# Three-layer graph network with a sign-split feed-forward stage: who fetches the last 128 rows of each group in layer 2, and who takes the signs

## The reference

```python
x = x + gnn(layernorm(x), edges, edge_type, W_rel, W_root, bias)
#   for l in range(3):
#       msg = einsum('nd,rde->rne', x, W_rel[l])[edge_type, src]
#       x = relu(segment_sum(msg, dst) + x @ W_root[l] + bias[l])
x = x + ffn(layernorm(x), weight, bias)
#   lx, lw = log(|x| + 1e-8), log(|w| + 1e-8);  mx, mw = their row maxima
#   log_out = log(exp(lx - mx) @ exp(lw - mw).T) + mx + mw.T
#   out = sign(sign(x) @ sign(w).T) * exp(log_out) + bias
```

## Time and profile before

| what | us |
|---|---|
| three timed runs | 5857.26, 5858.69, 5864.41 (median 5858.69) |
| profiled execution: time, span | 5867.15, 5865.4 |
| POOL busy | 4326.9 (74%) |
| PE busy | 4266.2 (73%) |
| VectorE busy | 1827.4 (31%) |
| ACT busy | 619.3 (11%) |

### The profile page before, as it was taken

How to read it: one execution, slowest core, us unless ns; L and a number is a source line. 1 busy time by engine, 2 the same in 40 slices (tenths; PEclk the granted TensorE clock), 3 DMA queues, 4 the chain that set the end, 5 groups by cost and what they waited for, 6 DMA issues and landing times.

```text
span 5865.4 us, 124620 instructions
## 1 busy us (share of the span) xinstructions
PE 4266.2 (73%) x26040; PEld 3874.6 (66%) x26041; DVE 1827.4 (31%) x3534; ACT 619.3 (11%) x848; POOL 4326.9 (74%) x4573
## 2 busy tenths in 40 slices
PE   3777777777777677777777777767777777777776
PEld 2766767666666566666666666656666666666666
DVE  4222222222222222222222222223333333334334
ACT  3010110101010010000000001001111111101111
POOL 4777777777777677777777777767777777777775
PEclk7999999999999898999999999989888888888898
DMA  6444444444444343444343334333334334333332
GB/s 194 116 117 116 118 117 116 117 117 117 117 117 116 108 114 112 113 113 113 112 113 113 113 112 114 112 103 113 113 113 115 113 112 114 113 113 113 113 113 85
DMA packets 314263, 674.98 MB, mean 115 GB/s; under 512 B 96052, under 2 KB 168217, under 8 KB 313850
## 3 DMA queue, kind: packets, MB, share of 16 engines
q0 software_dynamic: 218256, 596.28, 35.9%
q1 hardware_dynamic: 54580, 42.39, 2.5%
q10 hardware_dynamic: 41014, 32.79, 1.8%
HBM read 645.39 MB, written 25.68 MB: 114 GB/s over the span
## 4 chain that ended last, share of the span: by engine, by line
POOL 31%; PE 25%; issue 19%; SPq 13%; DMA 6%; DVEq 3%; DVE 2%; ACTq 1%; ACT 1%; POOLq 0%
POOL rows L452 31%; PE bank L473 14%; SPq L366 10%; PE bank L550 10%; DMA rows<-node_table,idx 5%; SPq L292 3%; DVEq L1110 1%; DVEq L1107 1%; DVE agg L1124 1%; ACTq L768 1%; DVEq L1214 1%; PE bank L689 0%; ACTq L292 0%; ACT agg L811 0%; ACT x_in L735 0%
## 5 line engine op out<-in xcount | busy, mean ns | idle before, releaser
L452 POOL DMA_INDIRECT rows<-node_table,idx x4547 | 4319.5, 950 | 1489.3 <-issue 1327.9
L473 PE MATMUL bank<-onehot,rows 128*128 128x128 f32 x18212 | 2658.6, 306 | 1227.7 <-DVE agg L1124 560.0
L473 PEld LDWEIGHTS bank<-onehot,rows 128*128 128x128 f32 x18212 | 2508.9, 218 | 1368.5 <-issue 1350.3
L1124 DVE TENSOR_TENSOR agg<-bank,agg 128x256 f32 x1566 | 664.0, 424 | 2111.6 <-PE bank L473 1578.8
L550 PE MATMUL bank<-wrel,agg 128*128 128x256 f32 x5568 | 1270.5, 387 | 16.5 <-issue 12.7
L550 PEld LDWEIGHTS bank<-wrel,agg 128*128 128x128 f32 x5568 | 1074.0, 196 | 167.5 <-issue 22.1
L1027 DVE TENSOR_TENSOR onehot<-bank,key 128x1152 f32<-128x1152 f32 x525 | 707.2, 1347 | 0.2
L811 ACT COPY agg<-zero_col 128x2304 f32 x174 | 367.2, 2111 | 2832.4 <-PE bank L550 1608.5
L1146 DVE SCALAR_TENSOR_TENSOR acc<-bank,in_first,acc 128x256 f32 x174 | 84.2, 484 | 1808.1 <-PE bank L550 1684.7
L818 ACT COPY acc<-bank 128x256 f32 (+1 forms) x98 | 36.5, 373 | 1224.9 <-issue 974.7
L663 PE MATMUL bank<-ident,new_x 128*128 128x128 f32 x196 | 43.1, 306 | 128.1 <-ACT new_x L869 128.1
(11 more groups left out here) (140 smaller groups left out, 864.2 us busy)
## 6 DMA issues: line engine op xcount, KB each, us to landing
far_rows<-node_table SPq DMA_DIRECT2D x12020, 1.0 KB
far_rows<-node_table ACTq DMA_DIRECT2D x6156, 1.0 KB
rows<-node_table,idx POOLq DMA_INDIRECT x4547
node_table<-new_x ACTq DMA_DIRECT2D x98, 128.0 KB
x_tile<-node_table SPq DMA_DIRECT2D x58, 128.0 KB
x_in<-in_x_dram SPq DMA_DIRECT2D x8, 768.0 KB, 11.2
wrel<-in_L_gnn_W_rel_dram SPq DMA_DIRECT2D x6, 1024.0 KB, 7.0
xres<-in_x_dram ACTq DMA_DIRECT2D x48, 128.0 KB
```

The costliest lines, as they stand in the source:

```text
L452: pool.indirect_dma_start(rows[:, s:s + D], None, tables[layer % 2], bass.IndirectOffsetOnAxis(ap=idx[:, g * TPG + k, j:j + 1], axis=0),). ...
L473: last = nc.tensor.matmul(to[:, h, :], row, hot[:, hot_k * CH + j, :], start=(j == 0), stop=(j == CH - 1))
L1124: nc.vector.tensor_tensor(window, seg[k % 3].rearrange("p h (r w) -> p h r w", r=R), window, ALU.add).then_inc(agg_added, 1)
```

## The change

The last gather of every group but a layer's last is now left out by POOL in layer 2 as well: SP fetches 74 of its rows and ACT 54, as in the other layers. ACT issues its 54 rows in one batch, in all layers, ahead of the work for a finished tile. ACT no longer takes the two signs nor copies the turned tiles. VectorE makes each sign from two instructions ((v > 0) - (v < 0)) and copies `magT` and `sgnT` behind triple 5.

```diff
@@ POOL, every group
-for j in range(CH - 1 if k == TPG - 1 and (layer < L - 1 or g % 2) else CH):
+for j in range(CH - 1 if k == TPG - 1 else CH):
@@ SP, layers 1 and 2
-    if layer < L - 1:
-        multiplied(layer, g)
-        for q in range(QUARTERS - 1):
-            fetch(layer, g, m % 2, q)
-    elif m % 2:
-        multiplied(layer, g)
-        for q in range(QUARTERS):
-            fetch(layer, g, 1, q, P)
+    multiplied(layer, g)
+    for q in range(QUARTERS - 1):
+        fetch(layer, g, m % 2, q)
@@ ACT, group
-if layer < L - 1:
-    fetch_ahead(layer, g, fetch_first)
+fetch_ahead(layer, g)          # all 54 rows
 if late:
     with act.If(g < late[0]):
         if layer < L - 1:
             next_sums(layer, late[1])
         else:
-            turned_tile(late[1])
             out_of_tile(late[1])
-if layer < L - 1:
-    fetch_ahead(layer, g, fetch_second)
@@ ACT, ended / out_of_tile
-nc.scalar.activation(sgn[:, :], z[:, :], ACT.Sign).then_inc(sgn_ready, 1)
-nc.scalar.activation(osgn[:, :], lns_sign_ps, ACT.Sign).then_inc(osgn_ready, 1)
@@ VectorE, group
+if late and k == TPG // 2 + 1:
+    with dve.If(g < late[0]):
+        turned_tile(late[1])
@@ VectorE, magnitudes
-link(t, 0, nc.vector.scalar_tensor_tensor(mag[:, :], z[:, :], -1.0, z[:, :], ALU.mult, ALU.max))
+link(t, 0, nc.vector.tensor_single_scalar(sgn[:, :], z[:, :], 0.0, ALU.is_lt))
+nc.vector.scalar_tensor_tensor(sgn[:, :], z[:, :], 0.0, sgn[:, :], ALU.is_gt, ALU.subtract).then_inc(sgn_ready, 1)
+link(t, 1, nc.vector.scalar_tensor_tensor(mag[:, :], z[:, :], -1.0, z[:, :], ALU.mult, ALU.max))
@@ VectorE, new
+def turned_tile(t):
+    dve.wait_ge(mag_transposed, t + 1)
+    dve.sem_inc(dve_mark, 1)
+    nc.vector.tensor_copy(magT[:, :, :], mag_ps).then_inc(magT_ready, 1)
+    nc.vector.tensor_copy(sgnT[:, :, :], sgn_ps).then_inc(sgnT_ready, 1)
@@ VectorE, result
-dve.wait_ge(osgn_ready, t + 1)
+dve.wait_ge(lns_ready, t + 1)
+link(t, 6, nc.vector.tensor_single_scalar(osgn[:, :], lns_sign_ps, 0.0, ALU.is_lt))
+link(t, 7, nc.vector.scalar_tensor_tensor(osgn[:, :], lns_sign_ps, 0.0, osgn[:, :], ALU.is_gt, ALU.subtract))
```

More of the change, by code:

```diff
@@ L361, in multiplied, with fetch @@
                     sp.sem_inc(sp_mark, 1)
-            def fetch(layer, g, b, q, rows=SP_ROWS):
-                first, end = q * LOADS, min(rows, (q + 1) * LOADS)
+            def fetch(layer, g, b, q):
+                first, end = q * LOADS, min(SP_ROWS, (q + 1) * LOADS)
                 for p, start in zip(range(first, end), far_starts(SP, g, q, 0, end - first)):
-                    sp.dma_start(far_row(p, b), far_from(layer, start)).then_inc(far_by_sp[layer][b][p // (rows // 2)], 16)
+                    sp.dma_start(far_row(p, b), far_from(layer, start)).then_inc(far_by_sp[layer][b][p // SP_HALF], 16)
             def first_layer(g, b, tile):
@@ L476, in far_landed @@
             def far_landed(layer, g, b):
-                if layer < L - 1:
[L478 to L486, removed]
+                pe.wait_ge(gathered[TPG - 1], g * (16 * (CH - 1)) + (layer * FETCHED + 1) * (16 * (CH - 1)))
+                for h in range(2):
+                    pe.wait_ge(far_by_sp[layer][b][h], g * (8 * SP_HALF) + (2 - b) * 8 * SP_HALF)
+                pe.wait_ge(far_by_act[layer][b], g * (8 * ACT_ROWS) + (2 - b) * 8 * ACT_ROWS)
             def rows_of(layer, g, k, b=None):
@@ L583, in group @@
                             pe.sem_inc(pe_mark, 1)
-                            products(seg[k % 3], rows, onehot[:, k // BATCH, :, :], k, k % BATCH, 0 if layer < L - 1 else None).then_inc(seg_ready, 1)
+                            products(seg[k % 3], rows, onehot[:, k // BATCH, :, :], k, k % BATCH, 0).then_inc(seg_ready, 1)
                         pe.sem_inc(pe_mark, 1)
@@ L764, in _, with fetch_part, multiplied @@
             act.wait_ge(far_at_ready, 1)
-            def fetch_quarter(layer, g, b, q, first):
-                for m, start in enumerate(far_starts(SCALAR, g, q, first, LOADS)):
+            def fetch_part(layer, g, b, q, first, end=LOADS):
+                for m, start in enumerate(far_starts(SCALAR, g, q, first, end)):
                     act.dma_start(far_row(q * LOADS + first + m, b), far_from(layer, start)).then_inc(far_by_act[layer][b], 16)
-            def fetch_first(layer, g, b):
+            def multiplied(layer, g):
                 if not isinstance(g, int):
@@ L774, in fetch_first, with fetch_rows, fetch_ahead @@
                     act.sem_inc(act_mark, 1)
[L775 to L780, removed]
+            def fetch_rows(layer, g, b):
+                multiplied(layer, g)
+                fetch_part(layer, g, b, QUARTERS - 2, SP_ROWS % LOADS)
+                fetch_part(layer, g, b, QUARTERS - 1, 0)
+            def fetch_ahead(layer, g):
                 with act.If(g < FETCHED - 1):
@@ L783, in fetch_ahead @@
                     with act.If(g % 2 > 0):
-                        part(layer, ahead, 0)
+                        fetch_rows(layer, ahead, 0)
                     with act.Else():
-                        part(layer, ahead, 1)
+                        fetch_rows(layer, ahead, 1)
                     act.sem_inc(act_mark, 1)
```

51 lines of the change are left out of this document (14 added, 37 removed).

## The result

The changed kernel took 5926.23 us (median of 4 runs, 5921.62 to 5930.94), the kernel before 5857.98 us beside it (4 runs, 5854.0 to 5864.41): a ratio of 1.0115 with a 95% interval of 1.0103 to 1.0128, so 68 us slower. The direction was forecast. The size wasn't: 5889 us stood in the prediction, and 5926 us lies above its range.

What follows compares the result with a forecast made beforehand. POOL paces layer 2, with the PE and VectorE loop only 72 us shorter. 101 us added to that loop, less 72.2 us of cover, plus 1.5 us at the end: +30 us, 5889 us; range 5845 to 5918 us.

Steps and rivals of the forecast that it cites:

- POOL's relief: 29 late groups of layer 2 each lose a gather: 36.4 us less POOL work, not on the path.
- The cover: Layer 2: PE waits 72.2 us for gathered rows, which hides that much added to the PE and VectorE loop.
- The sign of z: Two VectorE instructions ahead of `mag` delay the transposes by 0.84 us for each late group.
- The second sign: Sign of the sign product, two VectorE instructions ahead of `result` and the fold: 1.15 us (1.05 to 1.24) per late group.
- The copies: VectorE copies the turned tile behind triple 5's one-hot matrices: 0.1 us (0 to 0.25) per late group.
- The end: Behind the last group nothing runs beside the last tile; its signs add 1.5 us together.
- the sum for a late group: Both signs and copies lengthen layer 2's loop by 2.1 us (1.9 to 2.35), 101 us over 48 late groups.
- rival 2: TensorE's clock on triples 5 to 7: half faster, 5850 us, or a third slower, 5915 us; 18% and 8%.
- Fetches costed at nothing: SP's 74 and ACT's 54 rows for every layer 2 group cost nothing, hidden by the period.
- rival 3: ACT becomes late with the square root in late groups; 1 us each costs 48 us: 5937 us; 4%.
- Rival 1: POOL stays the bound in layer 2 and its 36 us are won: 5824 us; 12%.
- The rule weighed in the prediction: VectorE's new comparison of z would hold POOL up by up to 0.28 us per tile, some 14 us.

Runs made afterwards that it cites:

- VectorE parts alone: Kernel before plus VectorE's two signs and two copies, row fetches and gathers of layer 2 as before: 5874.27 us, ratio 1.0028.
- run with one instruction more: Kernel before plus VectorE's signs and copies and one small VectorE instruction ahead of the scaling of `mag`, fetches as before: 5939.23 us, ratio 1.012.

## Why the prediction was wrong

- **The mechanism held.** POOL's relief isn't on the path, PE's wait for gathered rows is 3.5 us (0 to 20 said), and POOL waits for PE (105 us where some 60 were said). Other groups take 27.31 us (27 said), late groups 35.74 us, just above the 33.5 to 35.5 said.
- **The cover.** The loop of a late group, its period without the last stage (the wait behind the fold), grew by 2.69 us. From the second transform to the last that is 48 x 2.69 = 129 us, of which 63.3 show: 66 us were covered (74 with the VectorE parts alone), 72 predicted. Right within 6 us.
- **The sign of z**: 0.84 us predicted, 0.79 measured. **The second sign**: 1.15 predicted, 1.17 measured. Right.
- **The copies**: 0.1 us (0 to 0.25) predicted. The stretch from transposes to product grew by 0.48 us, of which triples 5 to 7 are 0.31; 0.17 us remain for the copies. Within bounds.
- **The end**: 1.5 us predicted, 0.9 measured (28.0 against 27.1 us behind the last transform's start).
- **The term that failed** is the sum for a late group, "0.84 + 1.15 + 0.1 = 2.1 us (1.9 to 2.35)": it was 2.69 us, 129 instead of 101 us. It lacked two things, and some 0.07 us in the other stages. One is 0.18 us ahead of the transposes, most of it a delay that hangs on where VectorE's instructions stand in the program; no row of the kernel before shows it. The other is the slower clock of triples 5 to 7, 0.31 us. That was there as the harmful side of rival 2 ("if a third became slower, 5889 + 26 = 5915 us"), at 8%, kept outside the sum because its direction was open; in the event the groups with the short stretch fell from 15 to 7 of 48. The run with one instruction more shows how little moves it: 0.29 us in the wait ahead of the transposes, which the change was known to lengthen by 0.84 us. But the run with the VectorE parts alone, with the same 0.84 us, got better by 0.49 us (4.71 against 5.20), and the last 0.2 to 0.3 us turned that round. Which side it falls to could not be read from the rows of the kernel before. But I took half of the groups for the milder side and only a third for the harmful one, without a row for it; half on both gives 5889 + 39 = 5928 us, and the range should have reached there. Adding up: 5889 + 28 for the late groups + 6 for the smaller cover is 5923 us, of 5926 measured.
- **Fetches costed at nothing**: true of the change as it is, but for a reason that the prediction gave only half. That "what hides them is the period itself" held with ACT emptied: there ACT waits for VectorE's moments (224 us in layer 2) and isn't late. With its former work on ACT, in the order tried, they cost 4.3%. So rival 3 (ACT late) can happen, and VectorE's taking over kept it away.
- **Rival 1** (POOL stays the bound) is excluded: POOL waits 105 us for PE in the changed kernel. Already with the VectorE parts alone it is 1876.1 us from the second transform to the last, and POOL without any relief needs 56 x 26.5 x 1.257 = 1865 us for that. The loop was longer than that, so the 29 gathers had nothing left to give.
- **The rule weighed in the prediction.** The Trainium skill, "SBUF — State Buffer", section "Who interferes with whom", would by the prediction's estimate have the new comparisons hold POOL up by up to some 14 us in the layer. The window of the VectorE parts alone, below, has 1473 gathers where the earlier trace rows has 1472: nothing of it shows here.

```profile
3950.00:5800.00 1850.00, 1401.31 (x1473) 0.89 0.39 113
```

## What to carry to other kernels

Price a wait of PE by what PE does behind it, too: where matmuls run at 0.7 of the clock in some repetitions and at 1.0 in others, count how often each happens, and take both sides into the range, since a few tenths of a microsecond of idling moved 30 repetitions of 48 from one to the other here. Work for PE can be put into the wait: one triple ahead of the transposes, with `result` behind the fold, gave back the whole loss. What each of the two gave alone wasn't measured. Before costing work at nothing because the period hides it, add up the issuing engine's whole program for one period, in its order: what stands behind the new issues is what becomes late.

## What the runs showed of the hardware

- The granted clock of a stretch of 36 matmuls was 1.00 in one late group and 0.70 in another, 4.22 and 5.81 us. When PE's wait ahead of it grew from 2.67 to 3.05 us in the mean, the groups with the short stretch fell from 31 to 1 of 48. With a mean wait of 2.15 us (the kernel before) they were 15, so the wait's length is not the whole rule. The Trainium skill, "TensorE: Matmul & The Clock Gate", section "What's actually happening", says that idling halves the clock, and the two levels agree with the rows.
- The same two VectorE instructions start 565 ns apart, or 699 ns in nearly every repetition when they stand at one place of a long program; moved by three instructions the delay passes to the pair that is now there, moved by six it is no longer seen between these instructions. The Trainium skill, "Advanced Engine Details and Errata", section "ISA Cache", says that an engine's instructions are held in lines of 256. Whether the place is the edge of such a line no run here shows.
- The scaling of `mag` took 433 ns in the mean in the changed kernel and 362 to 365 ns in the kernel before, the VectorE parts alone and the kernel moved by six places, but 474 ns in the one moved by three. I have no cause for it.
- How fast SyncE and ACT issue fetches of single rows differs between sessions, and not by the chip's number: SyncE issued 230 or 123 rows in 100 us, and a kernel that leans on them takes 5.86 or 8.3 ms. The cause is open.
